# Between the score blocks and between the mixtures: moving TensorE work in an attention and in a local transformer

## The reference

```python
def local_attention(q, k, v):        # 16 heads of 64, windows of 32 tokens, each sees itself and the one before
    sim = einsum('bhwie,bhwje->bhwij', bq, look(bk)) * 8.0      # masked
    return einsum('bhwij,bhwje->bhwie', softmax(sim), look(bv))
def ffn_layer(x, g, bln, W1, b1, W2, b2):
    hg = layer_norm(x, g, bln) @ W1 + b1
    a, gate = split(hg, 2, -1)                                  # 341 wide each
    return a * gelu(gate) @ W2 + b2
x = attn_layer(shift_tokens(x), ...) + x     # q and k l2-normalised, scaled, rotated
x = ffn_layer(shift_tokens(x), ...) + x
```

```python
Q, K, V = rope(split(x @ Wq)), rope(split(x @ Wk)), split(x @ Wv)
scores = where(causal, Q @ K.T / sqrt(8), -inf)
out = (softmax(scores) @ V).merge_heads() @ Wo
```

## Time and profile before

| what | value |
|---|---|
| median of 3 runs | 5967.91 us |
| lowest, highest | 5953.04, 5971.70 us |
| the profiled execution | 6002.48 us |
| its span, first to last instruction | 6000.7 us |
| mean clock granted to TensorE | 0.901 |
| local transformer, steady part | 414 to 3720 us of the span |
| last attention, steps with value products | 5403 to 5822 us |

### The profile page before, as it was taken

One profiled execution on the slowest core, in us unless ns is written; L12 is line 12 of the kernel. 1 busy time (PEld: TensorE's weight loads), 2 busy tenths in 40 slices (PEclk: granted clock), 3 DMA queues, 4 the chain that ended last, 5 costly groups with the idle time before them and its releaser, 6 DMA issues. The chain is left out here.

```text
span 6000.7 us, 144359 instructions
## 1 busy us (share of the span) xinstructions
PE 4953.3 (83%) x57229; PEld 3437.5 (57%) x57263; DVE 3836.2 (64%) x9149; ACT 2872.2 (48%) x6252; POOL 2568.8 (43%) x3065
## 2 busy tenths in 40 slices
PE   7699999999999999999999997626499992458875
PEld 3366666666666666666666665425366661336653
DVE  7677767777677777777767774764377776443321
ACT  2366555656556565565656564201166663212221
POOL 4576666666666666666766663002200000000000
PEclk9899999999999999999999999757799996766667
DMA  0211111111111111111111010021100000000001
GB/s 19 68 29 25 31 32 27 24 32 30 27 26 32 30 26 24 33 33 27 23 32 27 19 23 19 6 63 41 36 1 1 2 1 3 19 19 20 20 16 38
DMA packets 312161, 150.56 MB, mean 25 GB/s; under 512 B 146143, under 2 KB 301003, under 8 KB 311243
## 3 DMA queue, kind: packets, MB, share of 16 engines
q1 hardware_dynamic: 309451, 137.20, 9.4%
q0 software_dynamic: 2048, 4.20, 0.3%
HBM read 101.10 MB, written 27.41 MB: 21 GB/s over the span
## 5 line engine op out<-in xcount | busy, mean ns | idle before, releaser
L1426 POOL TENSOR_TENSOR loc_a<-loc_a,loc_b 128x512 f32<-128x512 f32 x768 | 976.6, 1274 | 240.2 <-DVE loc_b L1502 239.1
L1123 PE MATMUL psum<-loc_wqk,loc_xt 128*128 128x512 f32 x1536 | 827.7, 621 | 18.2 <-issue 6.5
L1186 PE MATMUL psum<-loc_m,xn_rows 128*128 128x128 f32 x6144 | 830.4, 278 | 5.0 <-DVE y_rows L1534 2.7
L1302 ACT ACTIVATE loc_sq<-psum 128x512 f32<-128x512 f32 x768 | 455.1, 593 | 696.5 <-PE psum L1123 696.0
L1451 POOL TENSOR_TENSOR loc_a<-loc_a,loc_rn 128x512 f32<-128x512 f32 x768 | 785.2, 1045 | 0.1
L1186 PEld LDWEIGHTS psum<-loc_m,xn_rows 128*128 128x128 f32 x6144 | 751.9, 193 | 40.8 <-issue 38.1
L1498 DVE TENSOR_TENSOR loc_a<-psum,loc_rope 128x512 f32<-128x512 f32 x768 | 524.1, 682 | 336.9 <-ACT loc_sq L1302 315.6
L1458 POOL TENSOR_TENSOR xn_cols<-xn_cols,loc_rec 128x512 f32<-128x512 f32 x384 | 394.1, 1047 | 752.9 <-DVE loc_rec L1529 752.6
L1502 DVE TENSOR_TENSOR loc_b<-psum,loc_rope 128x512 f32<-128x512 f32 x768 | 521.8, 679 | 0.0
L1339 ACT COPY xn_rows<-psum 128x512 f32<-128x512 f32 x768 | 411.6, 588 | 226.1 <-PE psum L1174 222.3
L1506 DVE TENSOR_REDUCE loc_n<-loc_sq 128x8 f32<-128x512 f32 x768 | 518.0, 674 | 0.0
(11 more groups left out here) (365 smaller groups left out, 9120.1 us busy)
## 6 DMA issues: line engine op xcount, KB each, us to landing
loc_x<-loc_shifted SPq DMA_DIRECT2D x192, 256.0 KB, 4.0
loc_shifted<-y_rows SPq DMA_DIRECT2D x144, 64.0 KB
loc_wqk<-in_L_ffn_Wqkv SPq DMA_DIRECT2D x24, 256.0 KB, 3.7
x_rows<-y_rows SPq DMA_DIRECT2D x96, 64.0 KB
x_rows<-y_rows SPq DMA_DIRECT2D x96, 63.5 KB
moe_w<-in_L_ffn_W SPq DMA_DIRECT2D x16, 256.0 KB, 4.8
l3a_qk<-l3a_rot SPq DMA_DIRECT2D x16, 256.0 KB, 2.1
grp_w<-in_L_ffn_W SPq DMA_DIRECT2D x16, 256.0 KB, 2.9
```

The source lines that it names most:

```text
L1123: nc.tensor.matmul(ring("p", i, unit), xt[:, b % 2, t * P:(t + 1) * P], wqk[:, unit * 512:(unit + 1) * 512], start=True, stop=True).then_i ...
L1186: last = nc.tensor.matmul(y_bank[:, 0:P], u[:, i % 2, h // 2, h % 2, :], m[:, h, :], start=(h == 0), stop=(h == HEADS - 1))
L1302: nc.scalar.activation(sq[:, g % 2, :], ring("p", i, unit), ACT.Square).then_inc(sem["squared"], 1)
L1426: nc.gpsimd.tensor_tensor(part, part, b_[:, g % 2, :], ALU.add).then_inc(sem["added"], 1)
```

## The change

Three things, all of them order.

1. Local transformer, TensorE: `hidden` takes the chunk as an argument. Chunk 0 stands between the first piece of the mixture and the last quarter of the output product, chunk 1 between that and the second piece, chunk 2 behind it.
2. Local transformer, ScalarE: `gelus` becomes `gelu(q, c)`. GELUs 0 and 1 stand ahead of the copies of the second piece, GELU 2 behind; the table loads stand ahead of GELU 0 and behind GELU 2.
3. Last attention: the halves of the value products stand behind K0 and K1, their copies on ScalarE behind the exponentials of K0 and K1; `turn_divided` goes from behind K1 to behind Q2. The list of the two shared banks follows.

```diff
-                def hidden(q):
-                    pe.wait_ge(sem["cols_ready"], q + 1)
-                    for c, (c0, n) in enumerate(HID_CHUNKS):
+                def hidden(q, c):
+                    c0, n = HID_CHUNKS[c]
+                    if c == 0:
+                        pe.wait_ge(sem["cols_ready"], q + 1)
...
                     if now(3):
                         mix(n - 3, 0)
+                    if group_at(n, 12) is not None:
+                        hidden(group_at(n, 12), 0)
                     if n % 2 == 1 and n + 1 < TILES:
                         turn_x((n + 1) // 2)
                     if now(4):
                         project_out(n - 4, 3)
+                    if group_at(n, 12) is not None:
+                        hidden(group_at(n, 12), 1)
                     if now(3):
                         mix(n - 3, 1)
                     if starts(n, 3) is not None:
                         multiply_weights(n // NT)
                     if group_at(n, 12) is not None:
-                        hidden(group_at(n, 12))
+                        hidden(group_at(n, 12), 2)
...
+                def gelu(q, c):
+                    n, k = INS[c], CH * q + c
+                    if c == 0:
+                        nc.scalar.preload_act_table_set("gelu_and_others")
+                    act.wait_ge(sem["gate_done"], k + 1)
+                    if k >= 2:
+                        act.wait_ge(sem["h_ready"], k - 1)
+                    nc.scalar.activation(gel[0:n, k % 2, :], ring("gate", q, c)[0:n, :], ACT.Gelu,
+                                         bias=b1[0:n, 1, c:c + 1]).then_inc(sem["gelu_done"], 1)
+                    if c == CH - 1:
+                        nc.scalar.preload_act_table_set("natural_log_exp_and_others")
...
+                    if group_at(n, 12) is not None:
+                        gelu(group_at(n, 12), 0)
+                        gelu(group_at(n, 12), 1)
                     if now(3):
                         copy_mixed(n - 3, 1)
...
                     if group_at(n, 12) is not None:
-                        gelus(group_at(n, 12))
+                        gelu(group_at(n, 12), 2)
...
+                        if now(4) and b == 2:
+                            turn_divided(n - 4)
                         if now(2) and b == 2:
                             project_values(n - 2)
                         if now(2):
                             turned_scores(n - 2, b)
-                        if now(4) and b == 1:
-                            turn_divided(n - 4)
-                    if now(3):
-                        mix(n - 3, 0)
-                        mix(n - 3, 1)
+                        if now(3) and b < 2:
+                            mix(n - 3, b)
...
-                    if now(2):
-                        exps(n - 2, 0)
-                        exps(n - 2, 1)
+                    for b in range(2):
+                        if now(2):
+                            exps(n - 2, b)
+                        if now(3):
+                            copy_mixed(n - 3, b)
                     if now(4):
                         copy_divided(n - 4)
                     if now(2):
                         copy_values(n - 2)
                         exps(n - 2, 2)
-                    if now(3):
-                        copy_mixed(n - 3, 0)
-                        copy_mixed(n - 3, 1)
```

## The result

The changed kernel takes 5809.8 us (median of 4 runs, 5800.75 to 5818.85) against 5967.6 us (4 runs, 5953.04 to 5971.70): a ratio of 0.9742, 95% interval 0.9725 to 0.976, or 154 us less by the ratio. The profiled execution has a span of 5805.6 us and a mean clock of 0.920, where before it was 6000.7 us and 0.901. In one execution the program with the attention's change alone (second experiment) was in a slow state, at 10148 us, and its ratio leaves that one out.

The account below looks back on a forecast made before the run. TensorE bounds the local transformer; its queue order and clock bound the last attention. From a 5967.9 us median, -62 (local transformer) and -40 (last attention) make -102: 5866 us, range 5810 to 5945.

Parts of the forecast that it names:

- Local transformer, -62: Local transformer: reordered products and GELUs bring the next projection 1.3 to 1.4 us sooner a group, 62 us in all.
- Rival E: Local transformer: another chain (mixture 1 copies, a reload) returns the wait, 0 to +54 us: 5928 to 5982; chance 0.08.
- Last attention, waits: Last attention: moved value-product halves cover the waits for exponentials before Q1 and Q2, 2.3 us a step by waits alone.
- The new wait: Last attention, behind K2: TensorE waits at `turn_mixed` for two banks, some 1.5 us (0.6 at low clock).
- K0's wait: Last attention: K0's masks wait for the DMA of the maxima; 0.5 us of TensorE's waiting stays.
- The step with the clock up: Last attention: a step wholly at the high clock, waits included, takes 21.4 us.
- Last attention, clock: Last attention: where the clock falls and rises decides the size; 16 steps of 27.3 instead of 29.8 us save 40.
- so I expect it to fall there: Last attention: the clock falls at the emptiest place left, the wait behind K2, 1.5 us idle at one go.
- I take 27.3, between early and late: Last attention: the clock returns by half 0's end, a 27.3 us step, between 25.3 (up to K0) and 31.8 (Q2's masks).
- the early case: Last attention: the clock stays low only for the work up to K0, giving a step of 25.3 us.
- The price per low microsecond: Last attention: work takes some 1.82 times as long at low clock, so each us of high-clock work costs 0.82 more.
- rival A: Last attention: clock stays up for most of the step, saving 110 to 134 us there: 5772 to 5796; chance 0.10.

Follow-up runs that it names:

- the single piece with filler: The changed kernel with both value-product halves behind K1, plus two useless products between K0 and Q1: 5855.6 us, ratio 0.9802.

## Why the prediction was right and where it was wrong

**Local transformer, -62: right in mechanism and size.** Gate 0 at 1.06 (forecast 1.07), gate 1 at 4.30 (4.3), projection at 9.17 (9.1); 1.31 us a group where 1.37 was expected, 0.38 of wait for GELU 0 where 0.5 was. 1.31 x 45 is 59 us, and that part alone gave 61. (In the profiles the whole stage is 3436 to 3453 us in the five kernels with this order and 3507 to 3509 in three with the old one.) The load's start to GELU 0's start is 1.29 us, so no drain of 1.38 stands between; on this the trace differs from the Trainium skill, ScalarE: Activation LUTs, under what ACT_TABLE_LOAD costs, and the measurement decides. Rival E is out: no reload, 48 loads of each kind.

**Last attention, waits: right in size.** Both waits for exponentials went under the halves of the value products. The new wait is 1.63 (forecast 1.5), those for VectorE 0.46, 0.39 and 0.64 (forecast 0.5, for the maxima's DMA, and twice 0.3). K0's wait had the right size and the wrong releaser: only the weight load waited for that DMA, while the product ended its wait with VectorE's maxima, before as after (7.1 us in 13 times in both; line 2579 is 2587 after). The waits of before, 5403 to 5797 us:

```profile
PEld psum L2579 <- DMA l3a_qa<-l3a_top_rows: 10.0, 11, 1.7
PE psum L2579 <- DVE l3a_mx L2736: 7.1, 13, 1.5
```

The step with the clock up was put at 21.4 and takes 21.46, partly by luck: the terms written there (18.5 of work, 1.5, 0.5 and twice 0.3) add up to 21.1, and the waits are 0.5 longer than those. By waits alone the change is worth little: 2.3 us of them filled, 1.6 opened, some of it made up elsewhere.

**Last attention, clock: the step that failed.** The term was -40 and measured -93 (the part alone; its stage is 100 us shorter in the profiles, 418 instead of 519). It rested on "so I expect it to fall there", at the new wait, and on "I take 27.3, between early and late", 27.3 us a step between 25.3 and 31.8. Both halves of that were wrong. The clock falls in fewer steps, and at the new wait in three only: seven of the 13 take 21.4 to 21.6 us, with it up throughout. And where it falls it comes back early: in the stretches above 3.0 us at 0.50 take in the transposes and masks of Q0, and five steps of 23.0 to 24.5 result, less than even the early case. Only the last, of 27.0, has the length forecast, and not for the forecast reason: there the clock passes the new wait, falls behind one of 1.5 ahead of K0's masks and is back behind half 1. The price per low microsecond was right: the low level fell from 249 to 34 us of 13 steps, times 1 - 1/1.82 = 0.45 makes 97 us, and the 13 steps are (29.82 - 22.63) x 13 = 93 us shorter. The clock is the whole saving of this stage, and rival A, to which I gave 0.10, is nearly what happened; the measured 5810 lies 14 us above its upper end. That the time still touches the range is luck: its lower end adds 77 us of the local part, which gave 61, to 72 of the attention, which gave 93.

Why was it mis-sized? I took the long dense run of value products for what holds the clock up, and thought that taking it apart would cost. The runs show otherwise. What mostly brings the clock down in the kernel before is the 1.3 us wait behind K0: 12 of 13 falls stand behind it; filled with products whose result nobody reads, all else unchanged, it gives 0.86 instead of 0.68, and such products elsewhere give nothing. What remains of falls is shorter where dense products come sooner; that is read from the rows, no experiment has it by itself. The Trainium skill, TensorE: Matmul & The Clock Gate, in the section on a second failure mode, has the clock swinging with micro-idles between groups of products. The traces agree in kind (0.68 with two such waits, 0.86 with the first filled, 0.94 with both filled, although the last has a new one of 1.63), and I gave that too little weight.

**The size from run to run.** The profiled execution of before took 6002.5 us, the median 5967.6. Its stretches hold most of the 35, and not in the last attention: the local transformer took 3518 us where three other runs of the same order took 3507 to 3509, and from the first instruction of the experts stage to that of the next stage it is 386 where all others have 374 to 375. To make the sum against the median without scaling was right.

**Open.** Why a wait of 1.63 behind K2 lets the clock pass in some steps and not in others, and in nearly all while the 1.31 ahead of Q1 is open, why it falls at K1 behind a wait of 0.4, and why the single piece with filler has it low for 99 us of 13 steps and the halves for 34 to 65, isn't settled; no run here tells it apart. So the width of the wait just ahead does not explain every fall. A wait between K1 and Q2 alone was not filled by itself in the old order.

## What to carry to other kernels

When a stage's clock is below 1.00, read where it falls and what wait stands there before counting waits: here the change hardly altered TensorE's idle time, but the waits that it filled were those at which the clock fell, and that was worth 93 us. Useless products put into one suspected wait, with a control of the same products elsewhere, test this in two small edits. And in a hand-written order look for what the chain's last members have ahead of them in their own queue: taking a table load and a GELU out from behind two copies on ScalarE was worth 32 us, and one chunk of products out from ahead of a mixture 22. Take the clock from more than one profile: the same order had 34 us low in one and 65 in another.

## What was not expected of the hardware

Two added products of 128 x 256, 1.1 us a step, made the whole kernel 0.8% faster (ratio 0.9922) in a 1.3 us wait and 0.3% slower (1.0029) where there was none.

TensorE idles ahead of the second kind of score products (L1150) with "issue" as the end, that is, with no wait that the profile shows: 47 times and 68.6 us in the list above; over the whole stage it is 72.6 us in the changed kernel, 85.2 in the kernel before, and 73.8 to 81.0 in the ten others, with the same instructions in the same order in several of them. A difference of up to 10 us between two profiles of this stage is thus no effect of an edit.
